# Adapter tail: split operands for the second products, and the first selection turned earlier

## The reference

```python
logits = (x_flat @ Wr.T + br) / TEMPERATURE
probs = jax.nn.softmax(logits, axis=-1)
expert_idx = jnp.argmax(probs, axis=-1)
expert_weight = jnp.max(probs, axis=-1)
h = jnp.einsum('nd,erd->ner', x_flat, A)
y = jnp.einsum('ner,eor->neo', h, B) * SCALING
sel = jnp.take_along_axis(y, expert_idx[:, None, None], axis=1)[:, 0, :]
out_flat = sel * expert_weight[:, None]
...
x = x + out_flat
```

## Time and profile before

| | us |
|---|---|
| median of 3 runs | 626.66 (624.95 to 628.83) |
| the profiled execution | 628.45 |
| its span, first to last instruction | 626.3 |
| mean granted TensorE clock | 0.978 |
| FFN's last down product ends | about 592.2 |
| last PE instruction ends | 621.8 |

### The profile page before, as it was taken

One profiled execution on the slowest core, in us unless ns is written; L12 is line 12 of the kernel. 1 busy time (PEld: TensorE's weight loads), 2 busy tenths in 40 slices (PEclk: granted clock), 3 DMA queues, 4 the chain that ended last, 5 costly groups with the idle time before them and its releaser, 6 DMA issues.

```text
span 626.3 us, 13396 instructions
## 1 busy us (share of the span) xinstructions
PE 597.6 (95%) x5466; PEld 503.0 (80%) x5466; DVE 373.8 (60%) x668; ACT 340.2 (54%) x864; POOL 209.9 (34%) x222
## 2 busy tenths in 40 slices
PE   5889999999999989999998999999999998999996
PEld 3778888888888778888877888888788887788875
DVE  4775788778877666787855253262515376684553
ACT  0666687767776544544546453555445456556440
POOL 0671343444344623553434040131403025432000
PEclk8677999999999999999999999999999999999999
DMA  7760000000000129445101130112110001200024
GB/s 208 268 272 8 1 2 3 3 2 2 2 2 2 29 102 283 123 137 176 65 0 37 33 102 2 34 35 69 42 60 1 2 0 36 83 19 1 0 70 134
DMA packets 13676, 38.35 MB, mean 61 GB/s; under 512 B 2320, under 2 KB 3856, under 8 KB 13008
## 3 DMA queue, kind: packets, MB, share of 16 engines
q1 hardware_dynamic: 13376, 36.46, 17.7%
q10 hardware_dynamic: 240, 1.05, 0.7%
HBM read 36.39 MB, written 1.11 MB: 60 GB/s over the span
## 4 chain that ended last, share of the span: by engine, by line
PE 83%; DVE 6%; ACT 5%; DMA 3%; issue 2%; SPq 1%; ACTq 0%; POOL 0%; DVEq 0%
PE ps L1549 20%; PE ps L1551 18%; PE ps L1550 18%; PE ps L1667 8%; PE ps L1867 4%; PE ps L1626 3%; PE ps L1644 2%; PE ps L1656 2%; PE ps L1855 1%; DVE strm_lo L1381 1%; PE ps L1705 1%; DMA work<-in_cols 1%; PE ps L1578 1%; PE ps L2048 1%; ACT strm_hi L951 1%
## 5 line engine op out<-in xcount | busy, mean ns | idle before, releaser
L523 POOL TENSOR_TENSOR w_lo<-raw_w,w_hi 128x1024 fp32r<-128x1024 f32 x24 | 58.6, 2456 | 159.1 <-ACT w_hi L670 139.2
L1381 DVE SCALAR_TENSOR_TENSOR strm_lo<-ps,col,strm_hi 128x512 fp32r<-128x512 f32 x32 | 24.0, 751 | 104.3 <-ACT strm_hi L951 103.3
L1549 PE MATMUL ps<-w_hi,act_hi 128*128 128x512 f32 x160 | 65.3, 408 | 3.6 <-ACT junk L663 3.1
L936 ACT ACTIVATE work<-ps,col 128x512 f32<-128x512 f32 x64 | 43.9, 689 | 44.6 <-PE ps L1551 44.6
L1549 PE MATMUL ps<-act_hi,w_hi 128*128 128x512 f32 x160 | 63.6, 397 | 3.3 <-ACT work L936 1.9
L1551 PE MATMUL ps<-w_hi,act_lo 128*128 128x512 f32 x160 | 63.2, 395 | 0.0
L1550 PE MATMUL ps<-w_lo,act_hi 128*128 128x512 f32 x160 | 63.0, 394 | 0.0
L1551 PE MATMUL ps<-act_hi,w_lo 128*128 128x512 f32 x160 | 62.4, 390 | 0.0
L1550 PE MATMUL ps<-act_lo,w_hi 128*128 128x512 f32 x160 | 62.3, 389 | 0.0
L1667 PE MATMUL ps<-raw_w,xT 128*128 128x256 f32 x256 | 61.3, 380 | 0.0
L1667 PEld LDWEIGHTS ps<-raw_w,xT 128*128 128x128 f32 x256 | 46.3, 190 | 5.3
(11 more groups left out here) (202 smaller groups left out, 1437.0 us busy)
## 6 DMA issues: line engine op xcount, KB each, us to landing
raw_w<-in_w_attn SPq DMA_DIRECT2D x20, 512.0 KB, 3.5
raw_s<-in_w_moe SPq DMA_DIRECT2D x11, 384.0 KB, 5.3
work<-comb_dram SPq DMA_DIRECT2D x21, 128.0 KB, 2.9
raw_w<-in_w_qkv SPq DMA_DIRECT2D x4, 512.0 KB, 6.5
raw_w<-in_w_o SPq DMA_DIRECT2D x1, 2048.0 KB, 8.9
work<-comb_dram SPq DMA_DIRECT2D x8, 256.0 KB, 5.1
raw_s<-in_w_ffn SPq DMA_DIRECT2D x8, 256.0 KB, 2.8
bd<-in_w_ada SPq DMA_DIRECT2D x1, 1536.0 KB, 6.2
```

Of the source, the lines that this page charges most:

```text
L523: G.tensor_tensor(flat(w_lo[:, slot]), raw, flat(f32(w_hi[:, slot])), ALU.subtract).then_inc(s_piece_lo, 1)
L936: A(dst[:, h * BANK:(h + 1) * BANK], src, ACT.Identity, bias=c_(b, 4 * j + h)).then_inc(s_q1_copied, 1)
L1381: V.scalar_tensor_tensor(flat(strm_lo[:, n % SS]), ps[:, 4 + n % 2, :], c_("bv", 4 * UNITS[u][0] + h), flat(f32(strm_hi[:, n % SS])), ALU. ...
L1549: mm(dst, ah, bh, start=start and i == 0, stop=False, **flags)
```

## The change

- **Second products.** `lora_down` uses `split_mm`: the masked product hmk is split into act_hi (ACT, `hmk_hi`) and act_lo (VectorE, `share_lo`), in two slots. The masking product is now `share`, and waits for the low part three steps before in place of the product. The rows of B are split once, into the parts of slot 2 of w_hi and w_lo (`rows_hi`, `rows_lo`): ACT's four copies stand behind the FFN steps 13, 14 and 15, POOL's four subtractions at the end of its block.
- **Selection.** `router_pick(0)` stands between the two parts of `end_ffn(1)`. `turn_sel(0)` stands before up product 3, counted from 0, `logits1(1)` before 4 and `turn_sel(1)` before 7. ACT's queue follows that order, the parts of `x4_hi(1)` standing apart.
- **Adds.** The four residual adds stand behind all shares and low parts. Two of them wait for a new semaphore that counts the first bank of a half (`s_lora_sum`).

```diff
--- before.py
+++ after.py
...
@@ -384,6 +389,12 @@
 
         def z2_at(t):
             return hid[:, CT + t, :] if t < CT else z2[:, t, :]
+
+        rows_hi, rows_lo = (w[:, 2].rearrange("p a b -> p (a b)").rearrange("p (m n) -> p m n", m=MR) for w in (w_hi, w_lo))
+        ROWS = (0, MR - 1, 1, 2)
+
+        def rows_of(m):
+            return raw_t[:, 1, 2 * D:3 * D] if m == MR - 1 else raw_t[:, (MM + m) % SS, D:2 * D]
 
         LORA = [(m, c) for c in range(CHUNKS) for m in (0, 3, 1, 2)]
 
@@ -649,6 +660,9 @@
                             flat(f32(strm_hi[:, MM % SS, 2:4, :])), ALU.subtract).then_inc(s_slice_lo, 1)
             for m in (1, 2):
                 slice_lo(MI + MM + m + 1, MM + m, 2)
+            for i, m in enumerate(ROWS):
+                pool.wait_ge(s_rows_hi, i + 1)
+                G.tensor_tensor(rows_lo[:, m, :], rows_of(m), f32(rows_hi[:, m, :]), ALU.subtract).then_inc(s_rows_lo, 1)
 
 
         @block.scalar
@@ -1027,10 +1041,10 @@
             act.wait_ge(ld_tail, 32)
             A(flat(strm_hi[:, MM % SS, 2:4, :]), raw_t[:, 0, 2 * D:3 * D], ACT.Copy).then_inc(s_slice_hi, 1)
 
-            def x4_hi(c):
+            def x4_hi(c, parts=range(DK)):
 
                 s = slice(c * BANK, (c + 1) * BANK)
-                for m in range(DK):
+                for m in parts:
                     act.wait_ge(s_x4_ready, DK * c + m + 1)
                     A(act_hi[:, m, s], xT[:, m, s], ACT.Copy).then_inc(s_x4_hi, 1)
 
@@ -1055,14 +1069,34 @@
                 if n in (MM + 1, MM + 4):
                     m = 1 if n == MM + 1 else 2
                     slice_hi(MI + MM + m + 1, MM + m, 2)
+                if n >= NF - 3:
+                    act.wait_ge(s_ffn_down, MM + 2)
+                    for m in (ROWS[0:2], ROWS[2:3], ROWS[3:4])[n - NF + 3]:
+                        A(rows_hi[:, m, :], rows_of(m), ACT.Copy).then_inc(s_rows_hi, 1)
+
+            def hmk_hi(n):
+                act.wait_ge(s_hmk32, n + 1)
+                act.wait_ge(s_lora_up, MR)
+                if n >= 2:
+                    act.wait_ge(s_hmk_used, n - 1)
+                A(act_hi[:, n % 2, 0:BANK], hmk[:, n % 3, :], ACT.Copy).then_inc(s_hmk_hi, 1)
+
             router_exp(0)
             take_ups(0, 2)
-            x4_hi(1)
-            take_ups(2, MR)
+            x4_hi(1, (0,))
             take_selT(0)
+            take_ups(2, 3)
+            x4_hi(1, (1,))
+            take_ups(3, 4)
             router_exp(1)
-            take_ups(MR, NL)
+            take_ups(4, 6)
+            hmk_hi(0)
             take_selT(1)
+            take_ups(6, 7)
+            hmk_hi(1)
+            take_ups(7, NL)
+            for n in range(2, NL):
+                hmk_hi(n)
 
 
         @block.vector
@@ -1487,9 +1521,9 @@
                 V.scalar_tensor_tensor(rt[:, 9, g], rt[:, 7, g], 1.0 / RANK, over(rt[:, 4, g, 0], NE), ALU.mult,
                                        ALU.mult).then_inc(s_wsel, 1)
 
-            def end_ffn(c):
+            def end_ffn(c, parts=range(DK)):
                 dve.wait_ge(s_ffn_down, MM * (c + 1))
-                for m in range(DK):
+                for m in parts:
                     gated(ps[:, 2 * c + m, :], 5, "b2", c, m).then_inc(s_x4_ready, 1)
 
             def x4_lo(c):
@@ -1508,31 +1542,45 @@
                 if n == MM + 6:
                     router_shift(0)
             router_probs(0)
-            end_ffn(1)
+            end_ffn(1, (0,))
             router_pick(0)
+            end_ffn(1, (1,))
             x4_lo(1)
             router_shift(1)
             router_probs(1)
             router_pick(1)
 
-            def add_lora(c):
-
-                dve.wait_ge(s_hmk_used, MR * (c + 1))
-                for a in range(c * CT // 2, (c + 1) * CT // 2):
-                    t2 = slice(2 * a, 2 * a + 2)
-                    V.tensor_tensor(xres[:, t2, :], ps[:, (a + 2) % 4, :].rearrange("p (b n) -> p b n", b=2),
-                                    xres[:, t2, :], ALU.add).then_inc(s_y_ready, 1)
-
-            for n, (m, c) in enumerate(LORA):
+            def add_lora(a):
+
+                if a % 2 == 0:
+                    dve.wait_ge(s_lora_sum, a // 2 + 1)
+                else:
+                    dve.wait_ge(s_hmk_used, MR * (a // 2 + 1))
+                t2 = slice(2 * a, 2 * a + 2)
+                V.tensor_tensor(xres[:, t2, :], ps[:, (a + 2) % 4, :].rearrange("p (b n) -> p b n", b=2),
+                                xres[:, t2, :], ALU.add).then_inc(s_y_ready, 1)
+
+            def share(n):
+                m, c = LORA[n]
                 dve.wait_ge(s_up_copied, n + 1)
                 dve.wait_ge(ld_cb1[n], 32)
                 if n >= 3:
-                    dve.wait_ge(s_hmk_used, n - 2)
+                    dve.wait_ge(s_hmk_ready, n - 2)
                 V.tensor_tensor(hmk[:, n % 3, :], h1[:, n, :], cb1[:, m, c * BANK:(c + 1) * BANK],
-                                ALU.mult).then_inc(s_hmk_ready, 1)
-                if n == MR + 2:
-                    add_lora(0)
-            add_lora(1)
+                                ALU.mult).then_inc(s_hmk32, 1)
+
+            def share_lo(n):
+                dve.wait_ge(s_hmk_hi, n + 1)
+                V.tensor_tensor(act_lo[:, n % 2, 0:BANK], hmk[:, n % 3, :], f32(act_hi[:, n % 2, 0:BANK]),
+                                ALU.subtract).then_inc(s_hmk_ready, 1)
+
+            share(0)
+            for n in range(1, NL):
+                share(n)
+                share_lo(n - 1)
+            share_lo(NL - 1)
+            for a in range(TILES // 2):
+                add_lora(a)
 
 
         @block.tensor
@@ -2041,21 +2089,26 @@
             def lora_down(n):
                 m, c = LORA[n]
                 pe.wait_ge(s_hmk_ready, n + 1)
-                rows = raw_t[:, 1, 2 * D:3 * D] if m == MR - 1 else raw_t[:, (MM + m) % SS, D:2 * D]
+                pe.wait_ge(s_rows_lo, ROWS.index(m) + 1)
                 for t in range(CT):
 
                     bank = (2 * c + t // 2 + 2) % 4
-                    last = mm(ps[:, bank, (t % 2) * D:(t % 2 + 1) * D], hmk[:, n % 3, t * P:(t + 1) * P], rows,
-                              start=(n % MR == 0 and t % 2 == 0), stop=(n % MR == MR - 1), skip_group_check=True)
+                    own = slice(t * P, (t + 1) * P)
+                    last = split_mm(ps[:, bank, (t % 2) * D:(t % 2 + 1) * D],
+                                    [(act_hi[:, n % 2, own], act_lo[:, n % 2, own], rows_hi[:, m, :], rows_lo[:, m, :])],
+                                    start=(n % MR == 0 and t % 2 == 0), stop=(n % MR == MR - 1), skip_group_check=True)
+                    if n % MR == MR - 1 and t == 1:
+                        last.then_inc(s_lora_sum, 1)
                 last.then_inc(s_hmk_used, 1)
 
             for n in range(NL):
-                if n == 2:
+                if n == 3:
+                    turn_sel(0)
+                if n == 4:
                     logits1(1)
-                if n == MR:
-                    turn_sel(0)
+                if n == 7:
+                    turn_sel(1)
                 lora_up(n)
-            turn_sel(1)
             for n in range(MR):
                 lora_down(n)
             pe.wait_ge(s_selT_ready, CHUNKS)
```

More of the change, by code:

```diff
@@ L333, in build_program @@
         s_wsel = sem("wsel")
+        s_hmk32 = sem("hmk32")
+        s_hmk_hi = sem("hmk_hi")
         s_hmk_ready = sem("hmk_ready")
+        s_rows_hi = sem("rows_hi")
+        s_rows_lo = sem("rows_lo")
+        s_lora_sum = sem("lora_sum")
         block = ctx.enter_context(nc.Block())
```

## The result

| | before | after |
|---|---|---|
| median of 20 runs each, us | 628.01 (623.75 to 630.0) | 624.18 (620.38 to 627.43) |
| ratio, 95% interval | | 0.9959 (0.9941 to 0.9977) |
| profiled execution, us | 628.45 | 623.53 |
| its span | 626.3 | 621.6 |
| first adapters' up product starts | 592.16 | 589.23 |

What follows compares the result with a forecast made beforehand. The tail hangs on the first selection's copy and the second half's products behind the last broadcasts. Store 3.8 and second broadcasts 3.2 earlier, last product ending 619.5, then output issues: 2.2 less than 626.66, 624.5; range 622.0 to 627.8.

Steps and rivals of the forecast that it cites:

- fourth product: Second products on PE: the fourth starts at 612.0, its low part queued on VectorE behind share(4).
- The idle ahead of the fourth product: PE idles 1.75 because share_lo(3) stands behind share(4), which waits for the second broadcasts at 610.5.
- The halves of the constant rows: Splitting copies and subtractions in the last three FFN up products: priced at nothing, 0.4 without cover.
- the row of output issues: SyncE at the end: eight output DMAs from 618.55, the eighth issued at 621.8, limiting the saving to 2.2.
- The ring: Two act_hi/act_lo slots: 1.6 from a product's end to the next on its slot, so one product each 1.5.
- over 1.7 each: Sign of being wrong: the loop of the last four second products takes over 1.7 each; 1.5 was forecast.
- the early selection: First selection's turn on PE at 596.24, not 600.03; its store 3.8 earlier, the second broadcasts 3.2 earlier.
- 2.9 over all eight, if nothing feeds them slower: Split second products on PE: 1.43 instead of 1.79 for each m, 0.36 less, 2.9 over eight.
- The pick's place: router_pick(0) on VectorE after two of four residual instructions: ends by 595.3 instead of 596.52.
- The logits' place: Logits on PE moved behind up 3, at 598.0; up 2 begins at 594.88, where PE waited 0.31 for xT before.
- Rival (c): PE's clock falls behind the tail's added idle of 1.75: 626.0, or 631.3 if it stays low; chance 0.1.
- or if the stretch before 592 us differs at all: Sign of being wrong: any difference between the profiles in the part before 592 us.

Runs made afterwards that it cites:

- e3: The changed kernel with the first half's two residual adds moved ahead of the last low part on VectorE; tail 31.71 us, ratio 0.9943 to the kernel before.
- e1: The kernel before with only the changed order on PE, VectorE and ACT, second products still float32; tail 32.18 us, ratio 0.9956.
- e2: The changed kernel with the order of before restored, ACT's too, keeping the split products; tail 37.90 us, ratio 1.0057 to the kernel before.
- e7: The changed kernel with low part 3 ahead of share 4 and four operand slots instead of two; tail 30.40 us, ratio 0.9937 to the kernel before.
- e6: The changed kernel with the first pick behind both residual parts again, the turn still ahead of up product 3; tail 32.82 us, ratio 0.9975.
- f1: The kernel before with only the second half's logits moved behind up product 3, still ahead of the first turn; tail 32.78 us, ratio 0.9958.
- f2: The changed kernel with the second half's logits back ahead of up product 2; tail 38.88 us, ratio 1.0046 to the kernel before.
- e3 to e7: Includes two more runs on the changed kernel: low part 3 ahead of share 4 (tail 32.16, ratio 0.9962), and that plus early adds (31.23, 0.9933).

## Why the prediction was right

**Right by its steps.** 2.2 was forecast. The tail lost 1.3 to 1.8 over the four pairs of profiles with the full clock (34.14 and 34.04 before, 32.37 and 32.75 after); the ratio says 2.6 (1.4 to 3.7). In times behind the first up product, forecast and measured: first turn 4.08 and 4.09; store 5.3 and 5.34; the second pick in time for the second turn (at 601.06, without a wait); second store 13.2 and 13.08, its wait 1.6 and 1.47; spacing of the split products' instructions 0.119 and 0.119; fourth product 19.84 and 19.30; start of the last product (its forecast end less 1.5) 25.8 and 26.05; eighth output issue 29.6 and 29.97; end 31.9 and 32.4. The idle ahead of the fourth product was named with its cause. It came out at 1.0 and not 1.75, because the broadcasts landed 0.4 earlier and the third product ended 0.2 later; in the second profile it was 1.3. The halves of the constant rows, priced at nothing, cost nothing: PE had no wait at the first turn. e3 confirms the last step, the row of output issues: it gives back 0.66, where the sum by the two limits was 0.6.

**Where the closeness was luck.** Two terms were off and nearly cancelled. The fourth product came 0.54 earlier than forecast, but from it to the last it took 6.75 where four steps of 1.5 make 6.0, so the last came only 0.2 late. The ring was mis-sized: from the end of a product to the start of the next but one on its slot, 1.6 was put; the trace has 1.99 (third to fifth step, counted from 0) and 1.69 (fifth to seventh), and a product that starts behind a gap takes 1.53 or 1.54, not 1.43. The sign of being wrong, "over 1.7 each" for the last four, was thus at its edge: 1.74 between the starts of these four, 1.69 counted from the product before them. And 624.5 was built on a median before of 626.66; over the twenty runs it was 628.01, so the two medians differ by 3.8, and that the measured 624.18 lies so near to 624.5 is partly chance. The difference is the better test.

**The attribution was too even.** The text gave as its two levers the early selection and faster second products. e1 shows that the new order alone has all of the gain (32.18). e2 shows the split alone slower than before (37.90); part of that is the two falls of the clock, but the estimate without them (35.9) is still over 34.14. The 2.9 of shorter matmuls are real, but they are spent as idle of PE, between the low parts and the broadcasts. They pay only once the queueing and the ring are gone (e7, 30.40). The condition that failed was "2.9 over all eight, if nothing feeds them slower". That the sum came out right all the same is because it followed each wait, and did not count the 2.9 as gain.

**The pick's place was not priced.** The prediction tells the early turn from it. By its own rows the pick without the new place would have ended at 596.52, 0.3 behind PE's arrival at the turn at 596.24; by e6 the place is worth 0.45.

**The logits' place was priced too low.** The prediction names only their idle of 0.31, and f1's expectation took this alone. Moving them alone gives 1.36 of the 1.77 (f1). The store comes 0.77 earlier, not 0.31, and the later reads close the rest: PE's two halves run without a gap. From there the early selection adds little: in e1 the store is 3.05 earlier than in f1, but the tail is only 0.60 shorter, since in both all 64 instructions already run in one piece.

**Rival (c) was right in kind, but its decision by the idle alone was too narrow.** The changed kernel's clock stayed at 1.00 in both profiles; its longest idles, 0.82 and 1.16 by the profile, did nothing. The prediction let the length of the idle decide, somewhere between 1.4 and 3.09. The second fall of e2, behind 2.58 of idle with no logits near, fits that. Two of the three falls behind the logits do not: 0.31 of idle with 1.95 of 8-column logits right behind it brought one in one of three profiles of before, and 0.47 with the same in e2; the third, in f2, had 1.69. The rule that the prediction cites from the Trainium skill ("TensorE: Matmul & The Clock Gate", section "HAM oscillation") speaks of idle gaps. The trace agrees with it for the 3.09, and 2.58 brought the lower clock too; 0.31 and 0.47 are far shorter, and what these falls and f2's had in common was the small matmuls. In all nine profiles in which the logits stand behind up product 3, with no wait of PE right ahead of them (two of the change, e1, e3 to e7, f1), the clock was full. e6 has an idle of 0.33 with the four small matmuls of the turn behind it, and a full clock in its one profile. That the wait and the logits together are the cause fits all of these, but no run moved one without the other; it is not settled. Whether such falls count in the ratio is open too. The tail's 1.77 lies within the ratio's interval; a fall of 1.6 in a third of the executions before, and in none after, would add 0.5 to it. That is worked out, not measured.

**What doesn't belong to the change.** The first up product starts at 592.16, 589.13 and 592.06 in three profiles of before, and at 589.23 and 592.35 in two of the change. So the line "or if the stretch before 592 us differs at all" was a bad test. The difference of some 3 goes with the granted clock early in the program. In the first 60 us it is 0.77 in the first profile before and 0.89 in the first after, but 0.80 in the second after, by the windows of PE:

```profile
0.00:60.00 60.00, 47.72 (x599) 0.77 0.56 197
```

```profile
0.00:60.00 60.00, 44.50 (x642) 0.89 0.57 197
```

```profile
0.00:60.00 60.00, 47.01 (x612) 0.80 0.57 197
```

The stretch from 40 to 50 us parts them better: it has 0.83 in the five profiles of all kernels in which the first up product starts at 589.13 to 590.10, and 0.66 or 0.67 in the nine in which it starts at 590.50 to 592.97. It varies from one execution to the next, whichever kernel runs.

## What to carry to other kernels

Before a faster instruction is built in, ask what PE would do with the time: here PE waited for a chain of other engines, and a new order alone gave as much as the order and the faster products, with their two more handoffs, together. Look for small matmuls that wait for their operand: two up products later these had no wait, and where they stood the clock fell in some executions. When a stage is short against a kernel's spread, compare profiles from a mark inside the stage, not spans.

## What the runs showed of the hardware

- A product of float32 operands takes 0.224 for each of its two instructions of 256 columns (7.17 for 32); on fp32r parts one such instruction takes 0.119 (1.31 for eleven).
- The same 16 KB store took 1.46 to 1.88 until its landing released the next reads where the issue of the eight reads before it had ended 0.8 to 1.4 us earlier (the change twice, e1, e3 to e7, f2), and 1.99 to 2.53 right behind eight reads (before three times, e2, f1).
- After the granted clock fell behind the logits it was back some 3.5 us later in the second profile of before and in e2, but only after nearly 7 in f2.
- An idle of PE of 2.58 ahead of the second products was followed by the lower clock (e2); idles of 0.79 to 1.20 there were not (the change twice, e3 to e7).
